# Second attention: the first batch's sums, scaling, turns and loads moved to earlier slots, and the turns of q and k rows put at the end of their slots

## The reference, cut to what matters

```
xn = layernorm(x);  x = x + attention0(xn) * silu(ffn0(xn))       # layer 0
xn = layernorm(x);  x = x + attention1(xn) * silu(moe1(xn))       # layer 1

def attention1(x):                    # 16 heads of 16 features, 8 sequences
    q, k, v = x @ w_qkv.T             # (B, H, 256, 16) each
    q = q * rsqrt(mean(q*q) + eps) * q_norm_w      # root mean square over one head
    k = k * rsqrt(mean(k*k) + eps) * k_norm_w
    p = softmax(q @ k.T / 4)
    return (p @ v) @ w_proj.T + b_proj

def moe1(x):                          # 8 experts of width 176, the best 2 of each token; a shared expert of 352
    top2 of softmax(x @ router_w.T), normalised -> combine weights
    sum over experts of combine * (silu(x @ gate) * (x @ up)) @ down  +  the shared expert
```

## Time and profile before

| what | value |
|---|---|
| median of 3 runs | 1404.0 us (1403.33 to 1404.58) |
| profiled execution | 1404.14 us, of which 1402.3 us span |
| granted TensorE clock, mean over the span | 0.997 of full speed |
| TensorE busy | 1349.8 us, 96% of the span |
| TensorE weight loads | 1201.7 us (86%) |
| VectorE busy | 910.4 us (65%) |
| ACT busy | 752.8 us (54%) |
| GpSimd busy | 738.1 us (53%) |
| DMA | 190.78 MB, mean 136 GB/s |
| TensorE busy between 890 and 910 us | 16.19 of 20 us |
| TensorE busy between 910 and 930 us | 13.88 of 20 us |
| TensorE busy between 930 and 950 us | 17.56 of 20 us, mean clock 0.83 |
| between 1100 and 1200 us | TensorE 95.68, VectorE 79.30, GpSimd 68.82 of 100 us |

### The profile page before, as it was taken

The page is one execution under the profiler, slowest core; times in us unless marked ns, Lnnn a source line. Parts: engine busy times, 40 slices in busy tenths (PEclk is TensorE's granted clock), DMA queues, the critical chain, the costliest instruction groups (busy, mean ns, idle before and its releaser), DMA issues. The chain is left out here.

```text
span 1402.3 us, 25300 instructions
## 1 busy us (share of the span) xinstructions
PE 1349.8 (96%) x8758; PEld 1201.7 (86%) x8758; DVE 910.4 (65%) x1793; ACT 752.8 (54%) x1948; POOL 738.1 (53%) x725
## 2 busy tenths in 40 slices
PE   9999899999999999999999999879999999999898
PEld 7887798999899989998999898668888888889797
DVE  6655566556656665666565665557887777786765
ACT  4553444545544555445544544246666666666664
POOL 1651333554444545434645453448658676866775
PEclk9999999999999999999999999999999999999999
DMA  5995333324332343233324424166555653645572
GB/s 191 328 329 201 83 91 93 89 77 121 106 89 49 102 138 92 62 90 104 106 65 119 119 65 170 67 173 188 145 177 162 188 173 105 205 149 168 174 196 90
DMA packets 105645, 190.78 MB, mean 136 GB/s; under 512 B 20304, under 2 KB 39440, under 8 KB 103216
## 3 DMA queue, kind: packets, MB, share of 16 engines
q1 hardware_dynamic: 105520, 189.17, 45.0%
HBM read 116.68 MB, written 30.47 MB: 105 GB/s over the span
## 5 line engine op out<-in xcount | busy, mean ns | idle before, releaser
L775 POOL TENSOR_TENSOR a_pr<-a_pr,a_ri 128x512 f32<-128x512 f32 x128 | 133.2, 1041 | 299.5 <-DVE a_ri L955 299.5
L832 ACT ACTIVATE a_pr<-a_score,a_nb 128x256 f32<-128x256 f32 x256 | 119.0, 470 | 267.6 <-DVE a_nb L947 267.6
L1376 POOL TENSOR_TENSOR l_pr<-l_pr,l_ri 128x512 f32<-128x512 f32 x128 | 133.2, 1040 | 121.5 <-DVE l_ri L1728 119.5
L1487 ACT ACTIVATE l_pr<-l_score,l_nb 128x256 f32<-128x256 f32 x256 | 119.1, 471 | 107.7 <-DVE l_nb L1696 107.6
L58 PE MATMUL a_job<-s_xs,s_wh 128*128 128x512 f32 x384 | 153.8, 401 | 1.0 <-PEq L221 1.0
L60 PE MATMUL a_job<-s_xs,s_wl 128*128 128x512 f32 x384 | 151.7, 395 | 0.0
L59 PE MATMUL a_job<-s_xs,s_wh 128*128 128x512 f32 x384 | 151.3, 394 | 0.0
L947 DVE TENSOR_REDUCE a_nb<-a_score 128x2 f32<-128x512 f32 x128 | 88.5, 691 | 85.8 <-PE a_score L1026 84.1
L1696 DVE TENSOR_REDUCE l_nb<-l_score 128x2 f32<-128x512 f32 x128 | 87.5, 684 | 39.4 <-PE l_score L1836 39.2
L960 DVE TENSOR_TENSOR a_pt<-a_turn,a_pt 128x512 fp32r<-128x512 f32 x128 | 87.5, 684 | 23.7 <-ACT a_pt L840 23.7
L1495 ACT ACTIVATE s_wh<-l_turn 128x512 fp32r<-128x512 f32 x128 | 76.9, 600 | 36.3 <-PE l_turn L1846 36.3
(11 more groups left out here) (251 smaller groups left out, 4569.2 us busy)
## 6 DMA issues: line engine op xcount, KB each, us to landing
s_wl<-wgu_scratch SPq DMA_DIRECT2D x56, 512.0 KB, 5.7
a_sk<-a_rotk SPq DMA_DIRECT2D x384, 64.0 KB, 2.0
a_sq<-a_rotq SPq DMA_DIRECT2D x256, 64.0 KB, 2.0
s_xs<-xn_scratch SPq DMA_DIRECT2D x14, 1024.0 KB, 5.7
l_wd<-wd_scratch SPq DMA_DIRECT2D x56, 256.0 KB, 2.9
l_zq<-qs_scratch SPq DMA_DIRECT2D x128, 64.0 KB, 4.3
l_sk<-ks_scratch SPq DMA_DIRECT2D x32, 256.0 KB, 4.9
a_raw<-in_w SPq DMA_DIRECT2D x30, 256.0 KB, 3.0
```

What stands on the lines that cost most here:

```text
L775: pool.tensor_tensor(e, e, ri[:, n % 2, :].unsqueeze(2).broadcast_to([P, 2, SEQ]), ALU.mult)\
L832: i = act.activation(pr[:, n % 2, t, :], PS[n % 2][:, t * SEQ:(t + 1) * SEQ], ACT.Exp, bias=nb[:, n % 2, t:t + 1], accum_out=sm[:, n % 2, ...
L1376: pool.tensor_tensor(e, e, ri[:, n % 3, :].unsqueeze(2).broadcast_to([P, 2, SEQ]), ALU.mult)\
L1487: i = act.activation(pr[:, n % 3, t, :], PS[n % NPS][:, t * SEQ:(t + 1) * SEQ], ACT.Exp, bias=nb[:, n % 3, t:t + 1], accum_out=sm[:, n % 3 ...
```

## The change

Nothing is computed in another way. Four things move.

1. In the first batch the items X0 and X1 go from u = 9 and 10 to u = 7 and 8 (slots -9 and -8).
2. In every slot the items X0 or X1 are put behind the slot's other items.
3. In the first batch, the sums go from slots -12 and -11 to -14 and -13, the rounds of the root from -12..-10 to -13..-11, the weighting from -8 to -11, and the scalings from -9 and -8 to -12 and -11.
4. The loads of stack 0 and stack 1 go from slots -4 and 0 to slots -6 and -5 (`LOAD_AT`); the later stacks keep their slots.

```diff
--- before.py
+++ after.py
@@ -1089,7 +1089,7 @@
     UNIT, SLOT_GOAL, EARLY_GOAL = 10, 28.7, 18
 
     def X_AT(m):
-        return (9, 10)
+        return (7, 8) if m == 0 else (9, 10)
 
     def attn_jobs(n):
 
@@ -1124,6 +1124,7 @@
             while left and (credit >= cost(left[0]) / 2 or n == SLOTS[-1]):
                 credit -= cost(left[0])
                 ITEMS[n] = ITEMS[n] + [left.pop(0)]
+        ITEMS[n].sort(key=lambda item: item[0][0] == "X")
     for s in range(NSTEP):
 
         items = ITEMS[2 * H1 * s - 12]
@@ -1134,6 +1135,7 @@
     AT = {item: n for n in SLOTS for item in ITEMS[n]}
     ORDER = [("T", 0)] + [item for n in SLOTS for item in ITEMS[n] if item[0][0] not in "Dgul"]
     JOB = {item: i for i, item in enumerate(ORDER)}
+    LOAD_AT = {2 * PER_LOAD * i - 4 if i > 1 else i - 6: i for i in range(N // (2 * PER_LOAD))}
     U_AT = {n: [K for K in range(L) if AT["U", K] == n] for n in SLOTS}
     HID_AT = {n: [K for K in range(L) if AT["U", K] + 1 == n] for n in SLOTS}
     SUM_AT = {AT["D1", MT * (s + 1) - 1] + 1: s for s in range(NSTEP)}
@@ -1292,8 +1294,8 @@
                     m, u = n // H1 + 1, n % H1
                     if m < BATCH and u - 1 in X_AT(m):
                         store_stack(m, X_AT(m).index(u - 1))
-                    if n % (2 * PER_LOAD) == 0 and 0 <= n // (2 * PER_LOAD) + 1 < N // (2 * PER_LOAD):
-                        load_stack(n // (2 * PER_LOAD) + 1)
+                    if n in LOAD_AT:
+                        load_stack(LOAD_AT[n])
 
                 def store(s):
                     for i in range(2):
@@ -1405,9 +1407,10 @@
                 for n in SLOTS:
                     b, u = divmod(n, H1)
                     if b + 1 < BATCH:
-                        if u in (4, 5, 6):
-                            root_rms(b + 1, u - 4)
-                        if u == 8:
+                        first_root = 3 if b < 0 else 4
+                        if u in (first_root, first_root + 1, first_root + 2):
+                            root_rms(b + 1, u - first_root)
+                        if u == (5 if b < 0 else 8):
                             weigh(b + 1)
                         if u in (6, 11, 15):
                             spread(b + 1, (u - 6 + 1) // 5)
@@ -1711,13 +1714,14 @@
                     if 0 <= b and b + 2 < BATCH and u == 0:
                         norm_x(b + 2)
                     if b + 1 < BATCH:
-                        if u in ((4, 5) if b < 0 else (2, 3)):
-                            sum_squares(b + 1, u - (4 if b < 0 else 2))
+                        if u in (2, 3):
+                            sum_squares(b + 1, u - 2)
                         if u == 4 and b < 0:
                             dve.memset(zq[64:P, 0].bitcast(F32), 0.0).then_inc(S["zeroed"], 1)
                             dve.memset(zq[0:64, 1].bitcast(F32), 0.0).then_inc(S["zeroed"], 1)
-                        if u in (7, 8):
-                            scale_rows(b + 1, u - 7)
+                        first_scale = 4 if b < 0 else 7
+                        if u in (first_scale, first_scale + 1):
+                            scale_rows(b + 1, u - first_scale)
                     s, r = divmod(n + 12, 2 * H1)
                     if r in (1, 2, 3) and 0 <= s < NSTEP:
                         routing(s, r - 1)
```

## The result

The changed kernel takes 1408.0 us (median of 10 runs) against 1404.6 for the kernel before (10 runs): a ratio of 1.0026, 95% interval 1.0016 to 1.0036, some 3.6 us slower. The forecast was 1405.3, within 0.2% and thus "the same". The time is inside the stated range, but by the prediction's own mark of 0.2% it belongs to "slower" (0.31) and not to the likeliest case (0.48). The margin is small: the interval reaches down to 0.16%.

A forecast was written before the change was run, and what follows sets the result against it. TensorE, busy 96% of the span, was taken as the bound. The start of the second attention, +2.5 us, and the turns, -1.2, summed to +1.3 on 1404.0: 1405.3 us, with an 8 in 10 range of 1400.3 to 1409.5.

The forecast's parts named there:

- slower: Whole kernel: outcome slower than before by over 0.2%, given chance 0.31.
- the likeliest case: Whole kernel: time the same within 0.2%, given chance 0.48.
- The wait for stack 0 goes, that for gate load 5 comes: Start of second attention: first score's 5.0 us wait replaced by 4.8 us for gate load 5; tile 5 +2.2 us.
- the prediction's signs: Start of second attention: no key stack wait at the first score, then 4 to 6 us for gate weights.
- no stack is behind it in the new order, so 4.7: SP's queue at the start: gate load 5, issued at 930.0, takes 4.7 us to land, at 934.7.
- The rival with ct behind stack 1: Start: table store's landing waits for stack 1's key load; tile 5 after 936.2; +5.1 us, 1409.1; chance 0.28.
- VectorE ahead of the turns: First batch: VectorE waits 2.4 us for root steps, second scaling takes 1.7; first turned copy ends at 916.2.
- the early bound of 914.7: First batch: earliest end of the first turned copy, with quicker root steps and second scaling not slowed; -1.5 us.
- at no price: First batch: TensorE waits 2 us more ahead of the router's products, regained while VectorE is later; no cost.
- The clock behind the wait: Start: clock falls during the gate load wait; half speed costs 2.3 us instead of 2.05, +0.3.
- The turns at the end of their slots: Later batches: waits at turns go, partly moved to probabilities' turns; -1.2 us, bounds -4.9 and +2.8.
- Start: Start of second attention: tile 5 later by 2.2 us plus 0.3 for the clock, +2.5 us in sum.

The follow-up runs named there:

- e6: Changed kernel with VectorE's copy of the second turned x ahead of both sums of squares, first batch's scalings behind the V copy; 1406.8 us, ratio 1.0025 to before.
- e5: Kernel before, with turns of q and k rows behind their slot's other items in batches 1 to 7 alone; 1404.9 us, ratio 1.0007 to before.
- e9: Kernel before, turns last in batches 1 to 7 and their stores of turned rows called one slot later; 1401.7 us, ratio 0.9980 to before.
- e2: Changed kernel with items in the old order from slot 0 on, so only the first batch is changed; 1407.2 us, ratio 1.0020 to before.
- e3: Changed kernel with stack 1 loaded in slot -4 instead of -5, behind gate load 5; 1408.6 us, ratio 1.0027 to before.
- e4: Changed kernel with the first store of the combine table issued by ACT instead of SP; 1408.0 us, ratio 1.0022 to before.
- e12: Changed kernel, x copied first, first table stored by ACT, stack 1 in slot 0, later batches' stores one slot later; 1399.4 us, ratio 0.9965 to before.

## Why the prediction was right or wrong

**The wait for stack 0 goes, that for gate load 5 comes.** Right, with a wrong size. The forecast had the load issued at 930.0 and landed at 934.7; it was issued at 930.68 and landed at 936.8, and the wait was 8.3 us where the prediction's signs had 4 to 6. Of the 2.1 us between 934.7 and 936.8 some 0.4 are SP's wait for the table (3.22 us from ct to the gate load, 2.85 taken), 0.4 ct's own later issue (927.46, 927.1 taken), the rest the landing: 4.7 was taken from the earlier trace rows, 6.1 was the earlier trace rows and was measured. The term that failed was "no stack is behind it in the new order, so 4.7"; in all seven kernels above the load took 5.9 to 7.6 us, with and without a stack behind it.

**The rival with ct behind stack 1.** Its mechanism is what happened, at a smaller price: the key load of stack 1, issued at 926.85, landed after 3.2 us, at 930.05, and SP's next load went out at 930.28. The rival had put 5.5 for that landing. That an increment lands only after the earlier writes of its DMA engine is the rule of the Trainium skill which the prediction weighed ("DMA: Bandwidth & Descriptors", section "Queues, rings and completion order"); the trace agrees with it, to 0.23 us. By the prediction's own mark, tile 5 starting after 936.2, the outcome is this rival's and not the forecast's, though more of the lateness came from the load's landing than from ct.

**VectorE ahead of the turns.** The wait for the root steps came (1.77 us, 2.4 forecast), the second scaling was not slowed, and the first turned copy ended at 914.24 + 0.69 = 914.93, near the early bound of 914.7. VectorE in the changed kernel:

```profile
904.28 0.69 DVE L1638 TENSOR_TENSOR l_qk<-l_qk,l_rq 128x512 f32<-128x512 f32 x1 [1.77 <-POOL l_rq L1352]
...
906.30 0.68 DVE L1638 TENSOR_TENSOR l_qk<-l_qk,l_rq 128x512 f32<-128x512 f32 x1
...
914.24 0.69 DVE L1578 TENSOR_TENSOR l_tqk<-l_job,l_tqk 128x512 fp32r<-128x512 f32 x1 [0.31 <-ACT l_tqk L1462]
```

What the forecast had "at no price" was TensorE's wait at the router: it was 3.61 us, 2.7 more than the 0.89 before where the forecast had 2 more, and the clock fell in it. The mean clock is 0.66 between 898 and 900 and 0.78 between 908 and 910:

```profile
898.00:900.00 2.00, 0.00 (x0) 0.00 (x0) 1.93 (x5) 0.00 (x0) 0.29 (x1) 0.66 0.00 0
...
908.00:910.00 2.00, 2.00 (x8) 1.56 (x8) 1.82 (x7) 0.86 (x2) 0.53 (x2) 0.78 0.00 0
```

So TensorE worked at 1.2 GHz from 900.3 to 908.9 and came to the first turn at 911.74, 5.4 us after both scalings had begun. It, not VectorE, was the late one; e6 gets 1.5 us of that back at the stores.

**The clock behind the wait.** Forecast +0.3; the half speed behind tile 5's start lasted from 936.80 to 939.6 (mean 0.60 between 938 and 940), a loss of 1.4 in place of 2.05: -0.65.

```profile
938.00:940.00 2.00, 2.00 (x8) 1.61 (x8) 0.00 (x0) 0.27 (x1) 1.78 (x4) 0.60 1.05 330
```

**The turns at the end of their slots.** This is the step that failed. The forecast was -1.2, the runs show about +1.0. The waits at the turns went as forecast, and the waits at the turns of probabilities grew, by 5.8 us in all, more than the 4.9 that went. The working counted the instructions on TensorE, VectorE and ACT, and left out SP: the stores of turned rows wait for these turns at the head of SP's queue, and loads of combine weights stand behind them. In e5 the one behind batch 1's stores isn't issued later than before, but its issue takes 1.79 us and GpSimd waits 3.54 us for it; e9 takes that wait away by the place of the stores alone. Elsewhere the turns gained more than forecast: 0.7 + 2.1 us in e5.

**The sum.** Start +2.5 forecast, +2.8 measured (e2); turns -1.2 forecast, +1.0 measured; together +3.8 against 3.6 for the changed kernel. That the start came out near its forecast is in part luck: a landing 2.1 us later was set against 0.95 less lost to the clock than forecast (-0.65 in place of +0.3). The trace of e2 has head 5 at +3.7, that of the changed kernel at +5.1, and its ratio says 2.8, so the sum is not checked to better than a microsecond.

What stays open: why e3 and e4, in which tile 5 starts 3.9 and 4.6 us sooner from the first product of the stage, show nothing of it in their medians. In e3's trace the gain is lost again by head 18 (+6.3, as in the changed kernel's +6.5), in e4's it isn't (+1.4), and one trace each doesn't say which is usual.

## What to carry to other kernels

A move of work on one engine moves what other queues wait for: when an in-order DMA queue waits for the moved step, list what stands behind it in that queue, and give its place there the same thought as the step's own. Where the DMA engines are full, as between 928 and 936 us in the kernel before, an earlier issue of one load can be paid by another; order the loads by when they are wanted, and keep a queue from standing still behind a store that it waits for. And a gain that seems lost may be a good one with a bad neighbour: the kernel with the turns last was some 1 us slower than the kernel before, and 2.8 us faster once their stores had moved.

## What the runs showed of the hardware

An issue on SP's queue can itself take long: the same load of combine weights took 0.43 us to issue in e9 and 1.79 us in e5, right behind eight stores of turned rows and a down load. In the kernel before it took 0.44 us in that same place, and the gate load behind it 1.53. And the granted clock fell at different points of TensorE's waits: about 2.8 us into the idle time before 931.97 in the kernel before, about 4.3 us into that before 936.80 in the changed kernel (mean clock 0.60 from 932 to 936), but not within 3.19 us of idle time before 931.80 in e12; there it fell behind the wait, with TensorE at work:

```profile
928.00:932.00 4.00, 0.81 (x7) 0.64 (x6) 1.34 (x3) 1.08 (x4) 1.63 (x2) 1.00 1.00 321
932.00:936.00 4.00, 4.00 (x16) 3.48 (x16) 0.87 (x3) 1.69 (x5) 3.40 (x6) 0.57 1.04 289
```
